# The last layer of a two-layer model: one SiLU and the attention outputs change places with their neighbours in ScalarE's, PE's and VectorE's order

## The chip, the cores and the metric

The kernel runs on one core of a Trainium2 chip. The metric is the time of one execution on the device in microseconds, the median of three runs. The engines that matter here are PE (TensorE, matmuls), ScalarE (ACT), VectorE (DVE) and GpSimd (POOL). Each runs its own list of instructions in order and waits on semaphores for the others.

## The reference, cut to what matters

The model takes 16 x 128 tokens of width 256 through two layers. Layer 0 is a long convolution with gating and a mixture of 16 experts; the change does not touch it. Layer 1, the last, is an attention over features and a feed-forward layer with a low-rank part for each expert:

```python
scaled = einsum('bsd,bse->bde', q, k) / sqrt(256)        # q: the normalized x; k = v: the context
out = einsum('bde,bse->bsd', softmax(scaled, axis=1), v)
x = x + out
# feed-forward, x normalized; the two best of 8 experts (e0, e1), weights rw
for k in range(2):
    x1 = x @ W1.T + B1[e_k] @ (A1[e_k] @ x);  x3 = the same with W3, A3, B3
    x2 = silu(x1) * x3
    out = out + (x2 @ W2.T + B2[e_k] @ (A2[e_k] @ x2)) * rw[k]
x = x + out
```

## The kernel before, in words

`tail_phase` (line 1323) computes the last layer. The 2048 tokens are 8 groups of 256 tokens (two tiles of 128), and the 896 hidden features are 7 chunks of 128, so there are 56 chunk steps. All engines run through one list of steps S, from -7 to 59, with g = S // 7 and n = S % 7, and in each step they work on parts of several chunks. While the chunks of group g are computed, the attention and the routing of group G = g + 1 are spread over the same seven steps (`attention_group`, line 1312 and after). "Group G" below is always the group whose attention is worked on: group 1 in steps 0 to 6, group 2 in steps 7 to 13, up to group 7 in steps 42 to 48. Group 0 is done before the first chunk and the change does not touch it.

What a chunk F needs, with the lines of the profile's rows:

- PE: `base(F)`, 12 matmuls of L1438, products that both picks share; `low_rank(F, kind)`, 12 matmuls of L1453 for each of the two picks, which are added to the base products in the same PSUM bank (kind 0 in step F, kind 1, "the second kind", in step F + 1); `terms` (12 of L1485) and `down` (6 of L1499) in step F + 2.
- ScalarE: `silu(F, k)`, L1624; `hidden_high(F)`, the rounded parts hid_hi, L1630 and L1634.
- VectorE: `product(F, k)`, L1944; `hidden_low(F)`, the rests hid_lo, L1950.
- GpSimd: `weight(F, k)`, L1744; `both(F)`, L1749.

The matrices are split into a high and a low part. For the weights of the chunks of group 0 that happens in the first steps: `high_weights` on ScalarE (L1617) and `low_weights` on VectorE (L1819), two units in each of the steps 1 to 4. base(F) of the first group waits for 2 (F + 2) low units, so base(2) waits for unit 7, the first of step 1, and base(3) for unit 9, the first of step 2.

What group G adds to the steps:

- n = 0: PE `scores(G)` (L1525), n = 1: VectorE `find_top` (L1847), ScalarE `exponentials(G)`, four activations (L1656), VectorE `find_inverse` and `scale_context` (L1852, L1860), PE `attention_out(G)`, 8 matmuls (L1535), which wait for each tile's scaled context.
- n = 2: VectorE `masked_terms` (L1958, for the group whose chunks just ended) and `add_attention(G)` (L1867, then statistics L1872 and L1875); GpSimd `terms_sum` (L1760), `router_rstd(G)` (L1765, L1767), which waits for these statistics, then the step's gathers (`gathers`, L1724), then `weight(S-1, 1)` and `both(S-1)`; ScalarE `terms_high` (L1647), between silu(S-1, 1) and silu(S, 0); VectorE `terms_low` (L1963) and `router_input(G)` (L1884), both behind product(S, 0) and ahead of `hidden_low(S-1)`; PE `low_rank_out` (L1512), which waits for terms_low, and `turn(G)` (L1543), which waits for router_input.
- n = 3 to 6: transposed inputs, the router's logits, its picks and the expert masks.

masked_terms, terms_sum, terms_high, terms_low and low_rank_out exist only from step 9 on, so not in group 1. Exponentials and SiLU are in different activation tables; each change between them is an ACT_TABLE_LOAD, which has the line of the activation behind it.

The order of all of this is written out by hand in the five engines' loops over S. PE's wait for the second kind of chunk F is that product(F, 0) is done; base(F) waits for product(F - 2, 1), because it reuses the bank.

Of the kernel before, what the change touches and what calls it, by code (L numbers as in the profile page):

```python
# [1311 lines left out]
def low_units(S):  # L1312

    return {-6: (4,), -5: (5,), 0: (6,), 1: (7, 8), 2: (9, 10), 3: (11, 12), 4: (13, 14), 5: (15,)}.get(S, ())


def attention_group(S):

    group = S // FB + 1
    return group if 0 <= group < NG else None  # L1320


def tail_phase(nc, memory, a, stage, slots_dram, out_rows, ident, x_sb, comb_idx, norm, w_hi, w_lo, ctx_ring, banks):
# [33 lines left out]
    with ExitStack() as s:  # L1357
# [27 lines left out]
        def is_chunk(F):  # L1385
            return 0 <= F < LAST_CHUNK
# [34 lines left out]
        def _(pe):  # L1421
# [156 lines left out]
            for S in range(FIRST_STEP, END_STEP):  # L1578
                g, n = S // FB, S % FB
                G = attention_group(S)  # L1580
                if is_chunk(S) and S >= EARLY_BASE:
                    base(S)
                if is_chunk(S - 1):
                    low_rank(S - 1, 1)
                if is_chunk(S):
                    low_rank(S, 0)
                if n == 6 and G is not None and G > 0:
                    low_rank_in(G)
                if is_chunk(S - 2):
                    terms(S - 2, SECOND)  # L1590
                    terms(S - 2, BOTH)
                    down(S - 2)
                if n == 2 and 1 <= g <= NG:
                    low_rank_out(g - 1)
                if G is not None:
                    if n == 0:
                        scores(G)
                    if n == 1:
                        attention_out(G)
                    if n == 2:  # L1600
                        turn(G)
                    if n == 3:
                        logits(G)
                    if n == 3 and G == 0:
                        low_rank_in(0)
                        base(0)
                    if n == 5:
                        spread_picks(G)
                    if n == 5 and G == 0:
                        base(1)  # L1610

        @block.scalar
        def _(act):
            def high_weights(k):
                if k >= STAGE_SLOTS:
                    act.wait_ge(staged[k % STAGE_SLOTS], 16 * (k // STAGE_SLOTS))
                nc.scalar.copy(w_hi[:, W_CHUNK[k // 2], (k % 2) * W_COLS:(k % 2 + 1) * W_COLS],  # L1617
                               stage[:, k % STAGE_SLOTS, :]).then_inc(hi_split, 1)

            def silu(F, k):  # L1620
                act.wait_ge(second_done if k else first_done, F + 1)
                if F >= 2:
                    act.wait_ge(lo_done, 2 * (F - 1))
                nc.scalar.activation(f[:, F % 2, k, :], x_banks[F % 2][:, 0:GT], ACT.Silu).then_inc(silu_done, 1)  # L1624

            def hidden_high(F):
                act.wait_ge(weighted, 2 * F + 2)
                if F >= 2:
                    act.wait_ge(terms_done[SECOND], F - 1)
                nc.scalar.copy(hid_hi[:, F % 2, SECOND, :], f[:, F % 2, 1, :]).then_inc(hi_done, 1)  # L1630
                act.wait_ge(both_done, F + 1)
                if F >= 2:
                    act.wait_ge(down_done, F - 1)
                nc.scalar.copy(hid_hi[:, F % 2, BOTH, :], f[:, F % 2, 0, :]).then_inc(hi_done, 1)  # L1634

            def inputs_high(g, u):
                kind, w = u // 2, u % 2
                act.wait_ge(am_mul, 4 * g + u + 1)
                if g >= 1:
                    act.wait_ge(second_done if kind else first_done, FB * g)  # L1640
                nc.scalar.copy(am_hi[:, kind, w, :], mix[:, w, :]).then_inc(am_hi_done, 1)

            def terms_high(g):
                act.wait_ge(t_sum, g + 1)
                if g >= 1:
                    act.wait_ge(out_done, g)
                nc.scalar.copy(t_hi[:, :, :], mix[:, 0, :].rearrange("p (h t) -> p h t", h=HALVES)).then_inc(t_hi_done, 1)  # L1647

            def exponentials(G):
                for k in range(TG):  # L1650
                    b = TG * G + k
                    act.wait_ge(top_done, b + 1)
                    if G >= 1:
                        act.wait_ge(att_done, G)
                    for m in range(HALVES):
                        nc.scalar.activation(weights[:, k, m, :], att_banks[k][:, m * DIM:(m + 1) * DIM], ACT.Exp,  # L1656
                                             bias=minus_top[:, b, m:m + 1],
                                             accum_out=total[:, b, m:m + 1]).then_inc(exp_done, 1)

            def turned_copies(G):  # L1660
                act.wait_ge(turned, G + 1)
                if G >= 1:
                    act.wait_ge(logits_done, G)
                    act.wait_ge(x_low, G)
                nc.scalar.copy(x_t[:, :, :], att_banks[1][:, :].rearrange("p (c t) -> p c t", c=HALVES))\
                  .then_inc(xt_copied, 1)
                act.wait_ge(xt_copied, G + 1)
                if G >= 2:
                    act.wait_ge(second_done, FB * (G - 1))
                nc.scalar.copy(x_hi[:, G % 2, :, :], x_t[:, :, :]).then_inc(x_hi_done, 1)  # L1670

            def picks_copies(G):
                for kind in range(PICKS):
                    act.wait_ge(masks_spread, PICKS * G + kind + 1)
                    if G >= 2:
                        act.wait_ge(t_mul, 2 * (G - 1))
                    nc.scalar.copy(masks_sb[:, G % 2, kind, :], att_banks[kind][:, :]).then_inc(masks_copied, 1)
                act.wait_ge(rw_spread, G + 1)
                if G >= 2:
                    act.wait_ge(weighted, 2 * FB * (G - 1))  # L1680
                nc.scalar.copy(rw_sb[:, G % 2, :, :], out_banks[G % 2][:, :].rearrange("p (k t) -> p k t", k=PICKS))\
                  .then_inc(rw_copied, 1)

            nc.scalar.activation(warm[:, :], minus_half[:, 0:1], ACT.Exp)
            for k in range(STAGE_SLOTS):
                high_weights(k)
            for S in range(FIRST_STEP, END_STEP):
                g, n = S // FB, S % FB
                G = attention_group(S)
                if G is not None:  # L1690
                    if n == 1:
                        exponentials(G)
                    if n == 3:
                        turned_copies(G)
                    if n == 4:
                        act.wait_ge(exp_ready, G + 1)
                        nc.scalar.activation(probs[:, :, :], probs[:, :, :], ACT.Exp).then_inc(probs_exp, 1)
                    if n == 6:
                        picks_copies(G)
                if n == 0 and 0 <= g < NG:  # L1700
                    inputs_high(g, 0)
                    inputs_high(g, 1)
                if is_chunk(S - 1):
                    silu(S - 1, 1)
                if n == 0 and 0 <= g < NG:
                    inputs_high(g, 2)
                if n == 2 and 1 <= g <= NG:
                    terms_high(g - 1)
                if is_chunk(S):
                    silu(S, 0)  # L1710
                if n == 0 and 0 <= g < NG:
                    inputs_high(g, 3)
                if is_chunk(S - 1):
                    hidden_high(S - 1)
                for k in low_units(S):
                    high_weights(k)
# [88 lines left out]
        def _(dve):  # L1805
# [136 lines left out]
            def product(F, k):  # L1942
                dve.wait_ge(silu_done, 2 * F + k + 1)
                nc.vector.tensor_tensor(f[:, F % 2, k, :], f[:, F % 2, k, :], x_banks[F % 2][:, GT:2 * GT], ALU.mult)\  # L1944
                  .then_inc(prod_done, 1)
# [40 lines left out]
            for S in range(FIRST_STEP, END_STEP):  # L1986
                g, n = S // FB, S % FB
                G = attention_group(S)
# [10 lines left out]
                        find_top(b)  # L1999
                if n == 2 and after:  # L2000
                    masked_terms(g - 1)
                if n == 2 and G is not None:
                    add_attention(G)
                if n == 3 and after:
                    add_out(g - 1)
# [5 lines left out]
                    router_picks(G)  # L2011
                if is_chunk(S - 1):
                    product(S - 1, 1)
                if of_group:
                    inputs_product(g, 3)
                if n == 1:
# [95 lines left out]
```

## Time and profile before

| what | value |
|---|---|
| three runs | 795.66, 794.29, 795.27 us |
| median | 795.27 us |
| profiled execution | span 793.3 us from the first to the last instruction; no other time of it is given |
| mean granted TensorE clock | 0.956 of full |
| PE busy | 714.6 us (90%) |
| VectorE, GpSimd, ScalarE busy | 543.9 (69%), 443.1 (56%), 342.5 (43%) us |
| the last layer's chunk steps | from about 335 us to the end |

The span is 1.97 us below the median; what the profile shows is compared with its own span, and the difference is then applied to the median. Starts in the timelines are microseconds from the first instruction. Rows with xN merge N instructions of one form that lie side by side; the bracket at a row's end is the idle time of that engine before it and what ended it.

### The profile page before, as it was taken

Reading aid. Unit: us, or ns where it says so; the run is one execution under the profiler, and the core shown is the slowest. Engines: PE = TensorE matmul, PEld = TensorE weight load, DVE = VectorE, ACT = ScalarE, POOL = GpSimd, SP = SyncE. Lnnn points to the kernel's source line nnn. Section 1 sums busy time; section 2 is a strip of 40 time slices with the busy share of each in tenths; the row PEclk is TensorE's granted clock in tenths of the full one; section 3 lists DMA queues with packets and bytes.
Section 4 is the critical chain, followed back from the end, with each engine's and each line's share of the span. In section 5 each row is a group of like instructions: output and inputs, shape, how many; then the busy total and the mean of one; then the engine's idle time right before and its main releaser. Section 6 shows DMA issues by size and latency. Waiting matters only on the chain.

```text
span 793.3 us, 14732 instructions
## 1 busy us (share of the span) xinstructions
PE 714.6 (90%) x5217; PEld 652.3 (82%) x5217; DVE 543.9 (69%) x1278; ACT 342.5 (43%) x698; POOL 443.1 (56%) x532
## 2 busy tenths in 40 slices
PE   4899988959999981769899999999999999999996
PEld 2444567848999980658899999999999999999996
DVE  4999987975666644676667677677676586755533
ACT  2564533244666652164353344344444534443221
POOL 5877956047766605565276466474664773443532
PEclk9999998988999995689999999999999999999998
DMA  7675615946866864414012021020020110000000
GB/s 248 192 162 137 140 40 120 212 103 186 230 193 196 163 151 123 150 54 146 1 34 62 1 60 36 11 57 28 15 67 14 31 51 1 2 14 2 2 14 14
DMA packets 44599, 68.67 MB, mean 87 GB/s; under 512 B 7376, under 2 KB 32240, under 8 KB 44528
## 3 DMA queue, kind: packets, MB, share of 16 engines
q0 software_dynamic: 10080, 28.72, 17.0%
q1 hardware_dynamic: 34352, 38.97, 15.5%
q8 instruction: 44, 0.72, 0.4%
q14 instruction: 27, 0.22, 0.1%
q10 hardware_dynamic: 96, 0.04, 0.0%
HBM read 50.77 MB, written 14.84 MB: 83 GB/s over the span
## 4 chain that ended last, share of the span: by engine, by line
PE 52%; DVE 4%; POOL 3%; ACT 2%; issue 2%; POOLq 0%; DVEq 0%
PE psum L1453 19%; PE psum L1438 9%; PE psum L1485 9%; PE psum L1499 4%; PE psum L1471 2%; PE psum L1535 2%; PE psum L1525 2%; PE psum L1512 2%; POOL rows_back L1724 1%; PE psum L1553 1%; PE psum L1573 1%; DVE lora_w_lo L1819 1%; PE psum L1543 1%; ACT lora_w_hi L1617 0%; POOL hid L1744 0%
## 5 line engine op out<-in xcount | busy, mean ns | idle before, releaser
L1744 POOL TENSOR_TENSOR hid<-hid,rw_sb 128x256 f32<-128x256 f32 x112 | 93.3, 833 | 153.2 <-DVE hid L1944 152.9
L1453 PE MATMUL psum<-am_hi,lora_w_hi 128*128 128x256 f32 x448 | 127.4, 284 | 2.5 <-DVE am_lo L1939 2.2
L1453 PE MATMUL psum<-am_hi,lora_w_lo 128*128 128x256 f32 x448 | 127.2, 284 | 0.0
L1453 PE MATMUL psum<-am_lo,lora_w_hi 128*128 128x256 f32 x448 | 127.1, 284 | 0.0
L1944 DVE TENSOR_TENSOR hid<-hid,psum 128x256 f32<-128x256 f32 x112 | 46.8, 418 | 116.4 <-ACT hid L1624 115.2
L1624 ACT ACTIVATE hid<-psum 128x256 f32<-128x256 f32 x112 | 42.4, 385 | 177.2 <-PE psum L1453 177.0
L1043 POOL DMA_INDIRECT rows_in<-y_scratch,slot_token x80 | 76.2, 952 | 31.8 <-issue 27.1
L1724 POOL DMA_INDIRECT rows_back<-slots_scratch,comb_idx x64 | 66.6, 1040 | 39.8 <-POOLq L707 24.2
L1453 PEld LDWEIGHTS psum<-am_hi,lora_w_hi 128*128 128x128 f32 x448 | 85.9, 192 | 3.1 <-POOL am_lo L1755 3.1
L1950 DVE TENSOR_TENSOR hid_lo<-hid,hid_hi 128x256 fp32r<-128x256 f32 x112 | 74.1, 682 | 19.4 <-ACT hid_hi L1630 14.4
L1453 PEld LDWEIGHTS psum<-am_lo,lora_w_hi 128*128 128x128 f32 x448 | 86.0, 192 | 0.0
L1453 PEld LDWEIGHTS psum<-am_hi,lora_w_lo 128*128 128x128 f32 x448 | 85.9, 192 | 0.0
L1438 PE MATMUL psum<-lora_x_hi,lora_w_hi 128*128 128x256 f32 x224 | 67.7, 302 | 4.0 <-DVE lora_w_lo L1819 4.0
L327 POOL TENSOR_TENSOR kv<-ctx_t 128x1024 f32<-128x1024 f32 (+2 forms) x48 | 57.5, 1290 | 11.3 <-PE psum L448 11.3
L1485 PE MATMUL psum<-hid_hi,lora_w_hi 128*128 128x256 f32 x224 | 62.9, 281 | 0.7 <-DVE hid_lo L1950 0.7
L1438 PE MATMUL psum<-lora_x_lo,lora_w_hi 128*128 128x256 f32 x224 | 62.9, 281 | 0.0
L1438 PE MATMUL psum<-lora_x_hi,lora_w_lo 128*128 128x256 f32 x224 | 62.8, 280 | 0.0
L1485 PE MATMUL psum<-hid_lo,lora_w_hi 128*128 128x256 f32 x224 | 62.6, 279 | 0.0
L1485 PE MATMUL psum<-hid_hi,lora_w_lo 128*128 128x256 f32 x224 | 62.5, 279 | 0.0
L883 PE MATMUL psum<-moe_w_hi,moe_xt_hi 128*128 x160 | 49.5, 310 | 0.0
L1438 PEld LDWEIGHTS psum<-lora_x_hi,lora_w_hi 128*128 128x128 f32 x224 | 42.7, 191 | 5.2 <-DVE lora_w_lo L1819 4.8
L591 DVE TENSOR_TENSOR prod<-psum,q_t 128x1024 f32<-128x1024 f32 (+1 forms) x64 | 41.2, 685 | 8.2 <-PE psum L448 5.9
(255 smaller groups left out, 2147.7 us busy)
## 6 DMA issues: line engine op xcount, KB each, us to landing
slots_scratch<-y_out SPq DMA_DIRECT2D x40, 256.0 KB, 3.4
stage<-in_moe_weights SPq DMA_DIRECT2D x18, 384.0 KB, 3.7
moe_w_lo<-in_moe_weights POOLq DMA_DIRECT2D x18, 384.0 KB, 7.0
lora_stage_early<-in_lora_weights SPq DMA_DIRECT2D x16, 384.0 KB, 3.8
x_sb<-in_x SPq DMA_DIRECT2D x4, 512.0 KB, 6.1
ctx_t<-in_ctx_t SPq DMA_DIRECT2D x4, 512.0 KB, 7.4
y_scratch<-y SPq DMA_DIRECT2D x8, 256.0 KB, 2.6
x_sb<-shared_out POOLq DMA_DIRECT2D x4, 512.0 KB, 5.1
```

The source lines that it names most:

```text
L327: last = nc.gpsimd.tensor_tensor(kv[:, n % KV_SLOTS, :, first:first + shape[2] * shape[3]].rearrange("p n (i j) -> p n i j", j=shape[3]), ...
L591: last = nc.vector.tensor_tensor(prod[:, :, j, i], y_ji, query[:, :, i].unsqueeze(2).broadcast_to(shape), ALU.mult)
L883: last = nc.tensor.matmul(gu_banks[q % 2][:, k * DIM:(k + 1) * DIM], xp, wp, start=(c == 0 and j == 0), stop=(c == HALVES - 1 and j == 2))
L1043: nc.gpsimd.indirect_dma_start(out=rows_in[:, i % ROW_SLOTS, :], out_offset=None, in_=y_dram[:, :], in_offset=bass.IndirectOffsetOnAxis(ap ...
L1438: nc.tensor.matmul(x_banks[F % 2][:, w * GT:(w + 1) * GT], wp, xp, start=(w == 0 and c == 0 and k == 0), stop=False, skip_group_check=True)
L1453: last = nc.tensor.matmul(x_banks[F % 2][:, w * GT:(w + 1) * GT], wp, ap, start=False, stop=(half == 1 and k == 2), skip_group_check=True)
L1485: last = nc.tensor.matmul(term_banks[which][:, half * GT:(half + 1) * GT], wp, hp, start=(n == 0 and half == 0 and j == 0), stop=(n == FB ...
L1624: nc.scalar.activation(f[:, F % 2, k, :], x_banks[F % 2][:, 0:GT], ACT.Silu).then_inc(silu_done, 1)
L1724: nc.gpsimd.indirect_dma_start(out=rows_back[:, t % ROW_TILES, k * DIM:(k + 1) * DIM], out_offset=None, in_=slots_dram[:, :], in_offset=ba ...
L1744: nc.gpsimd.tensor_tensor(f[:, F % 2, k, :], f[:, F % 2, k, :], rw_sb[:, F // FB % 2, k, :], ALU.mult)\
L1944: nc.vector.tensor_tensor(f[:, F % 2, k, :], f[:, F % 2, k, :], x_banks[F % 2][:, GT:2 * GT], ALU.mult)\
L1950: nc.vector.tensor_tensor(hid_lo[:, F % 2, which, :], f[:, F % 2, 1 - which, :], hid_hi[:, F % 2, which, :].bitcast(FP32), ALU.subtract).t ...
```

## The change

On PE, `attention_out(G)` of groups 1 to 7 moves from the end of step n = 1 to step n = 2, behind base(S) and ahead of the second kind of the chunk before. On ScalarE, `exponentials(G)` of these groups move behind silu(S - 1, 1) in step n = 1. On VectorE, `add_attention(G)` moves behind product(S - 1, 1) in step n = 2. Group 0 keeps the old order. No instruction's size changes.

```diff
@@ PE
                 if is_chunk(S) and S >= EARLY_BASE:
                     base(S)
+                if n == 2 and G is not None and G > 0:
+                    attention_out(G)
                 if is_chunk(S - 1):
                     low_rank(S - 1, 1)
...
                     if n == 0:
                         scores(G)
-                    if n == 1:
+                    if n == 1 and G == 0:
                         attention_out(G)
@@ ScalarE
                 if G is not None:
-                    if n == 1:
+                    if n == 1 and G == 0:
                         exponentials(G)
...
                 if is_chunk(S - 1):
                     silu(S - 1, 1)
+                if n == 1 and G is not None and G > 0:
+                    exponentials(G)
@@ VectorE
                 if n == 2 and after:
                     masked_terms(g - 1)
-                if n == 2 and G is not None:
+                if n == 2 and G == 0:
                     add_attention(G)
...
                 if is_chunk(S - 1):
                     product(S - 1, 1)
+                if n == 2 and G is not None and G > 0:
+                    add_attention(G)
```

## Rows read from the trace of the kernel before

**Rows 1.** busy time in the stretch of steps 14 to 20 (columns: stretch, length, PE, PEld, DVE, ACT, POOL, PEclk, DMA share, GB/s)

```profile
455.00:510.00 55.00, 55.00 (x460) 54.36 (x459) 38.54 (x88) 23.43 (x51) 32.94 (x39) 1.00 0.12 35
```

**Rows 2.** timeline of PE, steps 1 to 5 (columns: start, us, engine, line, operation)

```profile
347.45 0.28 PE L1453 MATMUL psum<-am_lo,lora_w_hi 128*128 128x256 f32 x1
...
353.44 3.75 PE L1535 MATMUL psum<-att_weights,att_scaled 128*128 128x256 f32 x8 [4.15 <-DVE att_scaled L1860]
...
365.76 0.38 PE L1438 MATMUL psum<-lora_x_hi,lora_w_hi 128*128 128x256 f32 x1 [0.88 <-DVE lora_w_lo L1819]
...
374.23 0.38 PE L1438 MATMUL psum<-lora_x_hi,lora_w_hi 128*128 128x256 f32 x1 [1.07 <-DVE lora_w_lo L1819]
...
383.36 0.39 PE L1438 MATMUL psum<-lora_x_hi,lora_w_hi 128*128 128x256 f32 x1 [0.98 <-DVE lora_w_lo L1819]
```

**Rows 3.** timeline of ScalarE, steps 1 and 2

```profile
348.13 0.48 ACT L1656 ACTIVATE att_weights<-psum,att_minus_top 128x256 f32<-128x256 f32 x1 [0.73 <-DVE att_minus_top L1847]
...
350.08 1.28 ACT L1624 ACT_TABLE_LOAD   x1
351.37 0.66 ACT L1624 ACTIVATE hid<-psum 128x256 f32<-128x256 f32 x2
...
360.79 0.39 ACT L1624 ACTIVATE hid<-psum 128x256 f32<-128x256 f32 x1 [5.00 <-PE psum L1453]
```

**Rows 4.** timeline of VectorE, steps 1 and 2

```profile
352.32 1.84 DVE L1860 TENSOR_SCALAR att_scaled<-ctx_ring,att_inverse 128x128 f32<-128x128 f32 x4
...
355.62 1.82 DVE L1819 TENSOR_TENSOR lora_w_lo<-lora_stage_early,lora_w_hi 128x768 fp32r<-128x768 f32 x2
357.35 0.67 DVE L1867 TENSOR_TENSOR x_sb<-x_sb,psum 128x512 f32<-128x512 f32 x1
...
361.21 0.42 DVE L1944 TENSOR_TENSOR hid<-hid,psum 128x256 f32<-128x256 f32 x1 [2.18 <-ACT hid L1624]
...
362.98 1.19 DVE L1884 TENSOR_SCALAR lora_y<-x_sb,meanvar,rstd 128x256 f32<-128x256 f32 x2
```

**Rows 5.** timeline of GpSimd, step 2

```profile
359.12 0.23 POOL L1765 TENSOR_SCALAR rstd<-meanvar 128x2 f32<-128x2 f32 x1 [3.71 <-DVE meanvar L1875]
359.43 0.72 POOL L1767 TENSOR_TENSOR rstd<-rstd,minus_half 128x2 f32<-128x2 f32 x1
360.34 1.05 POOL L1724 DMA_INDIRECT rows_back<-slots_scratch,comb_idx  x1 [0.18 <-issue]
361.72 0.73 POOL L1744 TENSOR_TENSOR hid<-hid,rw_sb 128x256 f32<-128x256 f32 x1 [0.33 <-DVE hid L1944]
```

**Rows 6.** busy time and granted clock in three short stretches (columns as Rows 1)

```profile
351.75:352.00 0.25, 0.00 (x0) 0.00 (x0) 0.21 (x1) 0.25 (x2) 0.00 (x0) 0.61 0.84 328
...
358.50:359.00 0.50, 0.50 (x5) 0.50 (x5) 0.50 (x3) 0.00 (x0) 0.00 (x0) 0.87 1.05 381
...
375.50:376.00 0.50, 0.50 (x6) 0.50 (x5) 0.00 (x0) 0.48 (x2) 0.00 (x0) 0.70 0.76 190
```

**Rows 7.** timeline of PE, steps 15 and 16

```profile
471.22 1.89 PE L1535 MATMUL psum<-att_weights,att_scaled 128*128 128x256 f32 x8
...
474.32 0.28 PE L1453 MATMUL psum<-am_hi,lora_w_hi 128*128 128x256 f32 x1
...
479.29 0.28 PE L1512 MATMUL psum<-lora_w_hi,t_hi 128*128 128x256 f32 x1
```

**Rows 8.** timeline of ScalarE, step 16

```profile
475.94 0.39 ACT L1624 ACTIVATE hid<-psum 128x256 f32<-128x256 f32 x1 [3.94 <-PE psum L1453]
476.22 0.61 ACT L1647 CAST t_hi<-mix 128x512 fp32r<-128x512 f32 x1
```

**Rows 9.** timeline of VectorE, step 16

```profile
473.30 1.27 DVE L1958 TENSOR_TENSOR mix<-psum,masks_sb 128x512 f32<-128x512 f32 x2
...
478.13 0.99 DVE L1963 TENSOR_TENSOR t_lo<-mix,t_hi 128x512 fp32r<-128x512 f32 x1
```

**Rows 10.** timeline of GpSimd, step 16

```profile
474.65 1.29 POOL L1760 TENSOR_TENSOR mix<-mix 128x512 f32<-128x512 f32 x1 [1.56 <-DVE mix L1958]
```

## Prediction

> **What bounds the kernel now.** I read the page first: PE is busy for 714.6 of 793.3 us, and the chain that ended last is mostly PE's matmuls of the last layer. That says where the time is, not where the change can act, so I cut the last layer in two with the view of busy time by stretch and the timelines. From about 402 us PE never pauses: in the stretch of steps 14 to 20 it is busy for 55.00 of 55.00 us at the full clock [rows 1]. This holds for groups 2 to 7, six groups of seven steps. Taking a wait out there can bring nothing; putting one in costs its full length. Before 402 us, in group 1, PE does pause: 4.15 us ahead of the attention outputs, and ahead of each base(3), base(4), base(5) for VectorE's low weight parts (L1819) [rows 2]. Steps 1 to 6 are a ring: base(S) and low_rank on PE, SiLU, product, GpSimd's weight and both, the hid_hi and hid_lo parts, high_weights, low_weights, base(S + 1). Whatever is added to the ring in group 1 moves everything behind it.
>
> **Step 1, ScalarE and VectorE.** No operation is added or removed, and there are two table loads as before: exponentials, then SiLU, 1.28 us each. What moves: silu(0,1) may start when low_rank(0,1) ends, 347.45 + 0.28, so at 347.8 instead of 351.37 [rows 2, 3]. Behind it: 0.39 us, exp load 1.28, four exponentials with their accumulators 1.95 (348.13 to 350.08), SiLU load 1.28, silu(1,0). The exponentials end at 351.4, 1.35 us later than now; silu(1,0) ends at 353.1. VectorE's four scalings (1.84 us [rows 4]) wait for the exponentials and two reciprocals of some 0.1 us, and end at 353.5 instead of 354.16. What follows them, product(1,0) and the two hid_lo parts, takes 1.5 us (354.16 to 355.62), then the first low weight unit half of 1.82. So unit 7, the last that base(2) needs, is ready at 355.9 instead of 356.5.
>
> **Step 2, PE.** Now the attention outputs fill 353.44 to 357.2 while base(2) would be held for its weights until 356.5 anyway [rows 2, 4]. They are nearly hidden there. After the change PE is idle from 349.3 to 355.9, then base(2), then the outputs, then low_rank(1,1). The clock fell to the 1.2 GHz level at 351.85 after 2.5 us of idle PE and came back at about 358.6, 5.2 us after PE had resumed [rows 6]. At the full clock 42 matmuls take 4.97 us [rows 7], so the twelve of base(2) take 1.4, and the outputs 1.6 of their 1.89 until the next matmul starts; at the low one they take about 2.7 and 3.75. I take the clock back at the same moment, 358.6 (lower bound of the cold work: 2.7 us; upper: the 5.2 us seen). Then base(2) ends at 358.6, the outputs at 360.2, and silu(1,1) comes 1.62 us after low_rank starts (474.32 to 475.94 in step 16 [rows 7, 8]), at 361.8 instead of 360.79: 1.0 late, with bounds 0.5 and 2.3.
>
> **Step 2, VectorE and GpSimd: the largest term.** add_attention now stands behind product(1,1), but GpSimd's order is unchanged: router_rstd(1), one gather, and only then weight(1,1). From the addition to the first reciprocal-root instruction are 1.77 us (357.35 to 359.12), from there to the gather's end 2.27 (360.34 + 1.05 less 359.12) [rows 4, 5]. Today all that is over when product(1,1) ends at 361.63, and weight(1,1) follows at 361.72, 0.09 later. After: 1.77 + 2.27 and some gaps, 4.1 us later. Downstream 0.3 us is forgiven, because today the hid_lo parts of this step wait behind router_input (1.19 us from 362.98), which then fits under GpSimd's work. So base(3), now 4.13 us behind product(1,1), comes 7.8 behind it: +3.7. With the 1.0 above, base(3) moves from 365.76 to 370.5.
>
> **Steps 3 to 6.** PE now has two pauses before base(3), the longer some 3 us, so it will probably run at the low clock: silu(2,1) then comes up to 2.4 us later relative to base(3), of which about 0.8 was waiting on VectorE and GpSimd anyway: +1.5. Against that, the clock today falls at 375.65, just after base(4), and slows that step [rows 6]; base(4) to base(5) took 9.13 us against 8.47 for the step before [rows 2]. With PE fed almost without pause ahead of base(4), that is not repeated: -1.2. Step 5 is held by VectorE's router picks and moves along. Group 1: 1.0 + 3.7 + 1.5 - 1.2 = **+5.0 us**. Bounds: 3.0 (no cold stretch at base(3), the one at base(4) gone), 7.5 (the late clock in step 2 and at base(3), with nothing given back).
>
> **Groups 2 to 7.** Take group 3, steps 14 to 20; the others repeat it. In step 15 low_rank(14,1) starts at 466.25: the 42 matmuls from low_rank(15,1) at 474.32 to 479.29 take 4.97 us, and the same 42 lie before 471.22 [rows 7]. So silu(14,1) is ready at 467.87; with 0.39, 1.28, 1.95 the exponentials end at 471.5, the scalings at 472.6 for the first tile and 473.5 for the second. PE, having done base(16), asks for them at 472.6 and 473.5: at most 0.1 us lost. But VectorE is now late: product(15,0) and hid_lo until 475.05, so masked_terms starts there instead of at 473.30 [rows 9]. It takes 1.27, GpSimd's sum 0.08 later 1.29 [rows 10], the t_hi part 0.61 [rows 8], and silu(16,0) stands behind that on ScalarE, product(16,0) behind silu(16,0), t_lo (0.99) behind the product: 476.3, 477.7, 478.35, 478.65, 479.1, 480.0. PE wants it at 479.29 + 0.1; today it is ready at 479.12, so only 0.17 us of slack is there. A wait of 0.6. The router's z arrives at 481.1 to 481.6, when PE asks at 481.4: 0 to 0.2. I take 0.65 us for a group, bounds 0.3 and 0.9; six groups make **+3.9 us** (1.8 to 5.4). GpSimd's weight(15,1) also comes 2.4 us later, but terms(15) is due only after base(17) and two low_ranks, 5.6 us further on; that stays hidden.
>
> In this sum each switch of table costs one load, since SiLU starts 0.01 us after the load ends (350.08 + 1.28, then 351.37 [rows 3]). The Trainium skill, ScalarE: Activation LUTs, section What ACT_TABLE_LOAD costs, gives about 1.28 us for the load, with which the row agrees, and a drain of about 1.38 us behind it, which the rows don't show. By that rule a switch would cost 2.66 us and the sum would be some 15 us larger; the trace speaks against it.
>
> **Sum.** 5.0 + 3.9 = 8.9 us: the span goes from 793.3 to 802.2. The median of the runs, 795.27, is 1.97 above the span of the profiled execution, so I predict 804.2 us. A measurement of this kernel can tell about 0.2%, 1.6 us, from no change.
>
> **The rivals.**
> - *Group 1 alone loses.* If terms_low comes half a us sooner than I have it (its duration 0.7 instead of 0.99, masked_terms moved up), the slack of 0.17 suffices: 795.3 + 5.0 = 800.3 us. For it: I count every link at today's value under contention. Against: three links are fixed waits.
> - *The groups alone lose.* If GpSimd's late weight(1,1) falls into a wait that is there anyway, the time is 795.3 + 3.9 = 799.2. Against: base(3) waits for VectorE's weights today, so there is no such cover.
> - *The clock makes it dearer.* Every step of group 1 runs partly at 1.2 GHz: another 2.4 us in step 3 and 1.2 in step 4, together with the upper bound of the groups: 807 to 810 us. For it: a 4.15 us wait grows to 6.6.
> - *Dear switches.* Each of the two switches stops ScalarE for twice the length of a load, 2.56 instead of 1.28 us. Then in six groups the exponentials end 1.3 and silu(15,0) 2.6 us later than in my walk, t_lo follows, and PE waits about 2.4 us more in each: 804.2 + 14 = 818 us. Against it stand the 0.01 us between load and SiLU [rows 3]. The rule of the Trainium skill named above is what speaks for it.
> - *It does not matter.* Attention is off the chain and the new waits overlap with PE's pauses: 795.3. For it: in groups 2 to 7 the slacks are within half a us of enough. Against: group 1.
> - *Faster.* SiLU no longer stands behind exponentials, base(2) starts at 355.9 instead of 357.2, the outputs run at the full clock in 1.6 us instead of 3.75, and the cold stretch after base(4) vanishes: 0.3 us from the first two and 1.2 from the last, 793.8 us. It decides only if weight(1,1) is not held, that is if less than 1.5 of the 3.7 us reaches base(3), and if t_lo's slack suffices. The order in GpSimd's program speaks against it.
>
> **How the numbers follow.** Forecast as summed 0.62; group 1 alone 0.11; the groups alone 0.05; dearer clock 0.10; dear switches 0.01; no matter 0.07; faster 0.04. The likeliest case with its bounds goes from 800.0 to 808.2 (4.8 to 12.9 us added); to reach the groups-alone case I go down to 799.0, and take half of the dearer one with 809.0. Slower by over 0.2%: 0.62 + 0.11 + 0.05 + 0.10 + 0.01 = 0.89; same 0.07; faster 0.04.
>
> **What would show it.** In the profile after: a pause of PE ahead of base(2) of about 6.6 us, in place of 4.15 ahead of L1535; weight(1,1) (L1744) about 4.1 us behind product(1,1); base(3) near 370.5, base(5) near 388.5, and the first chunk of group 1 about 5 us late; the stretch of 55 us no longer full, with PE waiting about 0.6 us for t_lo (L1963) ahead of L1512 once in each of six groups; the chain passing through GpSimd and VectorE there. The forecast is wrong if weight(1,1) follows product(1,1) at once, if t_lo is ready before PE asks, or if PE's waits in group 1 shrink.

## The result, and the profile after

The changed kernel takes 804.03 us (median of 4 runs, 802.42 to 806.16) against 794.78 us for the kernel before on the same chip; the ratio is 1.0122, 95% interval 1.01 to 1.0145. The forecast was 804.2 us. By the medians the kernel grew by 9.25 us, where 8.9 were forecast on a median of 795.27. The profiled execution has a span of 802.5 us, 9.2 more than before. PE is busy for 715.8 us, 1.2 more than before, so nearly all of it is waiting.

Who PE waited for between 340 and 403 us, in the profile after:

```profile
PE psum L1438 <- DVE lora_w_lo L1823: 12.1, 5, 6.5
...
PE psum L1543 <- DVE lora_y L1888: 1.5, 1, 1.5
```

Before, PE's pause of step 1 ended with the scaled context [rows 2]; now there is none ahead of L1535, and the base matmuls wait 12.1 us in all for the low weight parts, 6.5 of them in one piece. The timeline of PE, steps 2 to 5:

```profile
356.10 0.58 PE L1438 MATMUL psum<-lora_x_hi,lora_w_hi 128*128 128x256 f32 x1 [6.50 <-DVE lora_w_lo L1823]
...
370.92 0.58 PE L1438 MATMUL psum<-lora_x_hi,lora_w_hi 128*128 128x256 f32 x1 [2.90 <-DVE lora_w_lo L1823]
...
381.11 0.38 PE L1438 MATMUL psum<-lora_x_hi,lora_w_hi 128*128 128x256 f32 x1 [0.41 <-DVE lora_w_lo L1823]
...
388.92 0.38 PE L1438 MATMUL psum<-lora_x_hi,lora_w_hi 128*128 128x256 f32 x1 [1.20 <-DVE lora_w_lo L1823]
```

base(3) is at 370.92, forecast 370.5; base(5) at 388.92, forecast near 388.5. The timeline of VectorE in step 2, which answers to [rows 4]:

```profile
362.75 0.42 DVE L1948 TENSOR_TENSOR hid<-hid,psum 128x256 f32<-128x256 f32 x1 [5.84 <-ACT hid L1626]
363.09 0.68 DVE L1871 TENSOR_TENSOR x_sb<-x_sb,psum 128x512 f32<-128x512 f32 x1
...
365.93 1.38 DVE L1888 TENSOR_SCALAR lora_y<-x_sb,meanvar,rstd 128x256 f32<-128x256 f32 x2 [0.85 <-POOL rstd L1771]
```

And of GpSimd, which answers to [rows 5]:

```profile
364.87 0.23 POOL L1769 TENSOR_SCALAR rstd<-meanvar 128x2 f32<-128x2 f32 x1 [9.97 <-DVE meanvar L1879]
...
366.08 1.05 POOL L1728 DMA_INDIRECT rows_back<-slots_scratch,comb_idx  x1 [0.18 <-issue]
367.17 0.73 POOL L1748 TENSOR_TENSOR hid<-hid,rw_sb 128x256 f32<-128x256 f32 x1
```

product(1,1) ends at 363.17. GpSimd has stood still for 9.97 us in front of router_rstd, then does that and the gather, and starts weight(1,1) at 367.17: 4.00 us behind the product, where it was 0.09.

To set the runs beside each other I use starts in the timelines of PE: of the first base matmul (base(0)), of base(2), of low_rank(1,1), of base(3), (5), (7), (49), and the end of the last matmul. What lies ahead of base(0) differs between two executions by a few us, whatever the kernel (base(0) at 333.0 to 339.0), so this length compares the edits better than the spans do. Each row of the table is one execution, the profiled one.

| us | base(0)-(2) | (2)-low_rank(1,1) | low_rank(1,1)-(3) | (3)-(5) | (5)-(7) | (7)-(49) | (49)-end | whole |
|---|---|---|---|---|---|---|---|---|
| before | 21.12 | 2.52 | 6.61 | 17.60 | 18.33 | 330.41 | 57.94 | 454.53 |
| after | 20.19 | 4.42 | 10.40 | 18.00 | 18.33 | 333.38 | 58.65 | 463.37 |
| only_group1 | 20.65 | 5.64 | 10.40 | 17.08 | 18.33 | 330.38 | 57.45 | 459.93 |
| only_groups | 21.52 | 2.05 | 6.81 | 17.82 | 18.32 | 332.20 | 57.36 | 456.08 |
| scalar_only | 20.89 | 2.50 | 6.60 | 16.24 | 18.32 | 337.89 | 57.36 | 459.80 |
| no_scalar | 20.73 | 4.45 | 10.40 | 18.00 | 18.31 | 334.05 | 57.35 | 463.29 |
| add_first | 20.26 | 4.35 | 8.24 | 17.18 | 18.32 | 332.16 | 58.34 | 458.85 |
| rstd_behind | 20.82 | 5.78 | 8.14 | 18.24 | 18.31 | 333.50 | 58.64 | 463.43 |
| gather_first | 20.96 | 5.63 | 9.15 | 17.17 | 18.37 | 336.27 | 58.60 | 466.15 |
| kept_busy | 20.32 | 3.03 | 10.43 | 18.15 | 18.36 | 333.31 | 58.10 | 461.70 |
| weights_first | 20.71 | 1.56 | 6.50 | 14.54 | 17.42 | 330.44 | 58.35 | 449.52 |
| weights_first_after | 20.32 | 4.52 | 8.26 | 15.98 | 17.36 | 335.01 | 58.66 | 460.11 |
| filled | 14.78 | 4.22 | 6.62 | 15.81 | 17.36 | 330.57 | 57.66 | 447.02 |

The whole grew by 8.8 us: 5.2 ahead of base(7), 3.0 from there to base(49), 0.7 behind it. The last column but one varies from 57.4 to 58.7 with no relation to the edits, so its 0.7 is not put down to the change.

What one execution can tell has limits. only_groups and add_first were profiled in the fastest of their six executions (794.62 and 797.79 us, medians 798.70 and 801.31), kept_busy, no_scalar and gather_first in their slowest. The kernel before has in its profile a low clock in step 4 (a mean of 0.50 from 376 to 378 us) which scalar_only and weights_first, with the same matmuls there, do not have (1.00 from 374 to 380 us); this is worth about 1.3 us (base(4) to base(5) 7.79 us in scalar_only, 9.13 before). So a stretch of the table shows a mechanism where the rows beside it do, and a difference of a microsecond or two of the whole needs the ratio of all executions.

### The profile page after: what moved, and what is told of

It reads as the page before. It is cut to its first block, busy times and chain, and to the rows that moved or that the text cites. A ratio compares the mean times of both kernels' runs of the same rounds, so it can differ in the third digit from the quotient of the medians.

```text
span 802.5 us, 14732 instructions
## 1 busy us (share of the span) xinstructions
PE 715.8 (89%) x5217; PEld 653.9 (81%) x5217; DVE 536.6 (67%) x1278; ACT 340.9 (42%) x698; POOL 445.3 (55%) x532
## 4 chain that ended last, share of the span: by engine, by line
PE 51%; DVE 5%; POOL 3%; ACT 2%; issue 1%; POOLq 0%; DVEq 0%
PE psum L1453 19%; PE psum L1438 10%; PE psum L1485 8%; PE psum L1499 4%; PE psum L1471 3%; PE psum L1525 2%; PE psum L1535 2%; PE psum L1512 1%; POOL rows_back L1728 1%; PE psum L1573 1%; DVE lora_w_lo L1823 1%; DVE lora_y L1888 1%; POOL rstd L1771 1%; PE psum L1553 1%; PE psum L1543 1%
## 5 line engine op out<-in xcount | busy, mean ns | idle before, releaser
L1748 POOL TENSOR_TENSOR hid<-hid,rw_sb 128x256 f32<-128x256 f32 x112 | 91.6, 818 | 154.3 <-DVE hid L1948 154.0
L1954 DVE TENSOR_TENSOR hid_lo<-hid,hid_hi 128x256 fp32r<-128x256 f32 x112 | 76.0, 695 | 28.5 <-ACT hid_hi L1632 22.2
L1438 PE MATMUL psum<-lora_x_hi,lora_w_hi 128*128 128x256 f32 x224 | 67.2, 300 | 12.1 <-DVE lora_w_lo L1823 12.1
L327 POOL TENSOR_TENSOR kv<-ctx_t 128x1024 f32<-128x1024 f32 (+2 forms) x48 | 57.4, 1289 | 11.4 <-PE psum L448 11.4
L1632 ACT CAST hid_hi<-hid 128x256 fp32r<-128x256 f32 x56 | 22.6, 403 | 58.6 <-POOL hid L1748 58.6
```

What stands on the lines that cost most here:

```text
L327: last = nc.gpsimd.tensor_tensor(kv[:, n % KV_SLOTS, :, first:first + shape[2] * shape[3]].rearrange("p n (i j) -> p n i j", j=shape[3]), ...
L1438: nc.tensor.matmul(x_banks[F % 2][:, w * GT:(w + 1) * GT], wp, xp, start=(w == 0 and c == 0 and k == 0), stop=False, skip_group_check=True)
L1748: nc.gpsimd.tensor_tensor(f[:, F % 2, k, :], f[:, F % 2, k, :], rw_sb[:, F // FB % 2, k, :], ALU.mult)\
L1954: nc.vector.tensor_tensor(hid_lo[:, F % 2, which, :], f[:, F % 2, 1 - which, :], hid_hi[:, F % 2, which, :].bitcast(FP32), ALU.subtract).t ...
```

## The experiments

The theory under test: group 1 loses because GpSimd's weight(1,1), part of the ring, waits behind router_rstd for statistics that now come late; the later groups lose a little because the router's z and t_lo come just too late. The main rival: the attention outputs on PE's path, and the low clock behind the longer pause, are the loss, and GpSimd's hold is hidden.

**only_group1 and only_groups: where it is lost.** In both, the conditions `G == 0` and `G > 0` of the changed kernel are altered on all three engines:

```diff
-                if n == 2 and G is not None and G > 0:
+                if n == 2 and G == 1:            # only_groups: G > 1
                     attention_out(G)
```

> The change for group 1 alone, groups 2 to 7 in the old order. Two terms theory: group 1 loses in its ring (base(3) near 370.9, scores(2) about 5.5 us later than before), PE waits for nothing in groups 2 to 7; about 5.5 us over the kernel before. If instead the loss were spread evenly over the seven groups: about 1.3 us.

> The change for groups 2 to 7 alone. Two terms theory: steps 0 to 6 as before (base(3) at 365.8), then 0.2 to 0.8 us in each of six groups ahead of low_rank_out and turn, 3.0 us in all, 798 us. If the six groups only passed on what group 1 did to the phase of the work: 795 us.

Measured: ratios 1.0083 (1.0054 to 1.0112) and 1.0071 (1.0048 to 1.0095). By the table only_group1 is 5.4 us longer than before, with (7) to (49) unchanged; only_groups leaves everything ahead of base(7) within a us and takes 1.8 us more in the six groups. The loss has two places. How it divides is less sure: by the medians only_groups costs 5.0 us (798.70 for 793.66; 3.8 to 7.5 by the interval), more than the 1.6 of its profiled execution, and only_group1 7.1, which together are more than the 9.25 of the whole change. In the profiles the six groups lose 1.8 us here and 3.0 with the whole change; a later section shows what these 1.2 us are.

**scalar_only and no_scalar: whose move it is.** scalar_only has the kernel before with ScalarE's part of the change, no_scalar the change without it:

```diff
+                if n == 1 and G is not None and G > 0:   # scalar_only; left out in no_scalar
+                    exponentials(G)
```

> Only ScalarE's part: exponentials(G) behind silu(S-1,1), PE and VectorE in the old order. The length from the first base matmul to the last matmul is 454.5 us before and 463.4 with the whole change. My theory: group 1 is as before or 0.4 us shorter (its ring is untouched), and in groups 2 to 7 PE, which asks for the scaled context 5.0 us after low_rank starts, gets it 5.9 after: 0.9 us a group; 459.8 us. If the later exponentials cost nothing without the other moves: 454.5.

> PE's and VectorE's part, exponentials where they were. My theory: GpSimd's hold in step 2 stays, so group 1 loses all of its 5 us (base(2) to base(3) 14 to 15 us instead of 9.1), and masked_terms is early again, so groups 2 to 7 lose at most 0.1 us each; 460 us by the same measure. If ScalarE's order were the cause in group 1: 455 to 457.

scalar_only: ratio 1.0094 (1.0073 to 1.0115), whole 459.80, the forecast figure. Its group 1 is even 1.6 us shorter than before, most of it between base(3) and base(5) (16.24 for 17.60), where the clock does not fall in this execution. PE's waits in its steps 8 to 48:

```profile
PE psum L1535 <- DVE att_scaled L1862: 5.2, 6, 0.9
```

The shape is as expected, though the six groups lose 7.5 us, not 5.4. The waits are 0.86 us in each group; t_lo took 1.31 or 1.32 us in groups 3, 4 and 6, which are 56.5 us long, and 0.68 to 0.73 in the others, which are 56.1. no_scalar: ratio 1.014 (1.0116 to 1.0163); group 1 has exactly the stretches of the whole change (4.45, 10.40, 18.00), so ScalarE's order has no part in that loss. But the six groups lose 3.6 us where I expected nearly nothing. Its waits there:

```profile
PE psum L1543 <- DVE lora_y L1886: 2.0, 5, 0.6
```

That is `turn`, which waits for router_input in five of the six groups: my expectation looked at t_lo and forgot that the later addition makes z late too.

**add_first, rstd_behind and gather_first: GpSimd's hold.** In add_first VectorE adds the attention in front of product(S-1,1), as before the change. rstd_behind does router_rstd(1) behind weight(1,1) and both(1). gather_first does the step's gather while GpSimd waits anyway:

```diff
 # add_first, VectorE
-                if n == 2 and G == 0:
+                if n == 2 and G is not None:
                     add_attention(G)
...
                     product(S - 1, 1)
-                if n == 2 and G is not None and G > 0:
-                    add_attention(G)
...
 # rstd_behind, GpSimd
                     both(S - 1)
+                if n == 2 and G == 1:
+                    router_rstd(G)
...
 # gather_first, GpSimd
+                if n == 2 and S >= 0:
+                    gathers(S)
                 if n == 2 and G is not None:
                     router_rstd(G)
...
-                gathers(S)
+                if n != 2 or S < 0:
+                    gathers(S)
```

> The change, but VectorE's add_attention stays ahead of product(S-1,1). My theory (GpSimd's weight(1,1) is held by router_rstd, which waits for the addition's statistics): add_attention now runs while PE does low_rank(1,1), weight(1,1) comes 1.3 us behind product(1,1) instead of 4.1, base(3) is 2.8 us earlier, and the router's z is in time in groups 2 to 7; 799.5 us, 4.5 less than the change. Rival (the attention outputs on PE's path and the low clock are the loss, GpSimd's hold is hidden): within 1 us of the change, 803 to 805.

> The change, but in group 1 GpSimd does router_rstd behind weight(1,1) and both(1). My theory: weight(1,1) follows product(1,1) at once (now 4 us later), the hid parts of this step are then held by VectorE's router_input instead, base(3) is 1.8 us earlier than with the change (33.2 instead of 35.0 us behind the first base matmul), and the whole 461.6 us. If GpSimd's order did nothing: 35.0 and 463.4.

> The change, with GpSimd's gather of step n = 2 ahead of router_rstd. It is then issued while GpSimd waits for the statistics. Group 1, my theory: weight(1,1) is held 1.25 us less, so from the first matmul of low_rank(1,1) to base(3) 9.2 us instead of 10.4. Groups 2 to 7: PE's wait for the router's z comes from VectorE's router_input, 0.73 us where GpSimd leaves it alone and 1.4 to 1.6 where they run side by side; with weight(S-1,1) now right beside it, it should be long in all six groups: steps 7 to 48 take 334.5 to 335.5 us instead of 333.4 (330.4 before the change). If the two engines don't slow each other, 333.4 or less, as GpSimd has less ahead of it.

The stretch from low_rank(1,1) to base(3) is the one in question. It is 10.40 us with the change, 8.24 in add_first, 8.14 in rstd_behind, 9.15 in gather_first (9.2 expected), 6.61 before. Three different edits of the hold each shorten it, and the rival, which needed it unchanged, falls as the explanation of this stretch. In rstd_behind weight(1,1) follows its product at once, 0.08 us behind it:

```profile
362.28 0.74 POOL L1748 TENSOR_TENSOR hid<-hid,rw_sb 128x256 f32<-128x256 f32 x1 [8.59 <-DVE hid L1950]
```

The 1.5 us that are left there above the 6.61 are VectorE's: router_input, which waits for router_rstd, ends at 366.10 us, and hidden_low(1) and the low weights stand behind it. The ratios: add_first 1.0095 (1.0072 to 1.0119), rstd_behind 1.0105 (1.008 to 1.013), gather_first 1.0138 (1.011 to 1.0166). Their intervals overlap with that of the whole change (1.01 to 1.0145), so it is the traces that show the effect of the hold, not the times of the kernel. The gain does not reach the whole in full. In rstd_behind it is lost again: base(2) to low_rank(1,1) is 5.78 instead of 4.42, because the attention outputs there ran at the low clock for 3.40 us instead of 2.04, and base(2) came 0.6 late:

```profile
356.49 3.40 PE L1535 MATMUL psum<-att_weights,att_scaled 128*128 128x256 f32 x8
```

only_group1 and gather_first show the same 1.2 us, with no edit there that could cause it (gather_first's is behind it). In the profile after, the granted clock is back at 359.1 us, 3.0 behind the start of base(2); in only_group1 it is back at 361.1, 5.5 behind. So when the clock comes back, relative to the work, is different from one profiled execution to the next, and is worth over 1 us in this stretch. rstd_behind as a whole (463.43) therefore missed its 461.6.

**The router's z, and VectorE beside GpSimd.** gather_first lost 5.9 us in the six groups, which I had expected to be 4.1 to 5.1; I had counted 1.4 to 1.6 us for router_input. Its router_input and GpSimd's work beside it, in the timelines of group 3:

```profile
486.20 1.63 DVE L1891 TENSOR_SCALAR lora_y<-x_sb,meanvar,rstd 128x256 f32<-128x256 f32 x2 [0.62 <-POOL rstd L1771]
```

```profile
486.14 0.73 POOL L1748 TENSOR_TENSOR hid<-hid,rw_sb 128x256 f32<-128x256 f32 x1
486.95 0.73 POOL L1753 TENSOR_TENSOR hid<-hid 128x256 f32<-128x256 f32 x1
```

It took 1.62 or 1.63 us in all six groups. In the changed kernel the same two instructions, with a gather beside them, take 0.73 us in groups 2, 3 and 5 and 1.39, 1.39 and 1.63 in groups 4, 6 and 7; the timelines of VectorE, groups 3 and 4:

```profile
485.83 0.73 DVE L1888 TENSOR_SCALAR lora_y<-x_sb,meanvar,rstd 128x256 f32<-128x256 f32 x2 [0.62 <-POOL rstd L1771]
...
541.10 1.39 DVE L1888 TENSOR_SCALAR lora_y<-x_sb,meanvar,rstd 128x256 f32<-128x256 f32 x2 [0.62 <-POOL rstd L1771]
```

And what PE waits for `turn` in group 4:

```profile
542.54 0.65 PE L1543 MATMUL psum<-ident,lora_y 128*128 128x128 f32 x4 [0.33 <-DVE lora_y L1888]
```

From base to base, groups 2 to 7 of the changed kernel take 55.28, 55.27, 55.78, 55.24, 55.79 and 56.02 us, against 55.05 (55.19 in the last) before: 0.2 us where router_input is short, 0.7 to 0.8 where it is long. In only_groups five of six are short, which are the 1.2 us between 1.8 and 3.0. It is not group 1 that decides: with group 1 changed too, rstd_behind has three long ones and weights_first_after six. What decides between short and long with a gather beside it was not found out.

**kept_busy: the clock.** 52 matmuls without use ahead of base(2) and 22 ahead of base(3), written to banks that are free at that time:

```diff
+                if S == 2:
+                    pe.wait_ge(am_mul, 4)
+                    keep_busy(term_banks[0], 52)
                 if is_chunk(S) and S >= EARLY_BASE:
                     base(S)
...
                         turn(G)
+                        if G == 1:
+                            pe.wait_ge(x_added, 2)
+                            keep_busy(att_banks[0], 22)
```

> The change, with 52 matmuls without use in PE's pause ahead of base(2) and 22 in the one ahead of base(3), so that the clock stays up. My theory: base(2) and base(3) still start when VectorE's weights are there (356.1 and about 369.6), but run at the full clock; low_rank(1,1) ends 1.3 us sooner, low_rank(2,1) another 1 to 1.5; 801.5 us, 2.5 less than the change. Rival (the clock is most of group 1's loss): 5 us less, 799. If the clock is nothing: 804.

The ratio is 1.0128 (1.0107 to 1.0149), no gain that can be seen in the times. In the profile base(2) to low_rank(1,1) is 3.03 instead of 4.42, the 1.4 us expected. The second part came to nothing: the clock stayed up at base(3) and fell a step later instead, in the stretch 381 to 387 us:

```profile
381.00:387.00 6.00, 5.43 (x33) 5.43 (x34) 2.00 (x6) 3.42 (x5) 0.00 (x0) 0.72 0.23 68
```

so (3) to (5) is 18.15 instead of 18.00. In this execution the clock was 1.4 us of group 1's length; it is not the loss, since the stretch from low_rank(1,1) to base(3) stayed at 10.43.

**weights_first, weights_first_after, filled: the ring, and a faster kernel.** If group 1 is a ring through the weight parts, these should be moved out from behind the hid parts:

```diff
+                for k in low_units(S):
+                    low_weights(k)          # and high_weights likewise on ScalarE
                 if is_chunk(S - 1):
                     hidden_low(S - 1)
-                for k in low_units(S):
-                    low_weights(k)
```

> The kernel before the change, with high_weights ahead of hidden_high on ScalarE and low_weights ahead of hidden_low on VectorE. My theory: group 1 is a ring through the weights, so taking them out from behind the hid parts shortens each of steps 2 to 6 by 0.5 to 1.2 us; 3 us less in all, 451.5 us by the same measure, about 791.5 for the kernel. If PE's pauses in group 1 have another cause: no gain.

> The whole change, and the weight parts ahead of the hid parts as in weights_first. From the first matmul of low_rank(1,1) to base(3) are 6.6 us before the change, 10.4 with it, 8.1 to 8.2 with GpSimd's hold shortened in either way. My theory (the hold costs because the ring through the weights passes behind the hid parts): with the weights out of it only router_input stands before them, 7.8 us; from the first base matmul to the last matmul 457.5 us instead of 463.4. If the hold reached base(3) by another way: 10 us again.

weights_first, made of the kernel before, has a ratio of 0.9969 (0.995 to 0.9988) and is 5.0 us shorter by the table, 3.1 of them between base(3) and base(5). About 1.3 of these, as much as in scalar_only, are the low clock of step 4 that this profile does not have, and by the medians the gain is 2.1 us. In weights_first_after, made of the changed kernel (ratio 1.0061, 1.0039 to 1.0083), the stretch from low_rank(1,1) to base(3) falls from 10.40 to 8.26, expected 7.8. The whole is 460.1 and not 457.5; 1.6 of the difference is router_input, which was long in all six groups (335.01 for 333.38). filled adds, for group 1 alone, the order of the change where it fits: units 7 and 8 are split ahead of everything in step 1, silu(0,1) comes before the exponentials, base(2) before the attention outputs, and add_attention stays in its old place.

```diff
 # ScalarE; VectorE has low_weights behind product(0, 1)
+                if S == 1:
+                    for k in low_units(S):
+                        high_weights(k)
...
                     silu(S - 1, 1)
+                if S == 1:
+                    exponentials(1)
 # PE
                     base(S)
+                if S == 2:
+                    attention_out(1)
```

> weights_first, and in group 1 alone what was sound in the change: silu(0,1) ahead of the exponentials and the attention outputs behind base(2), but with units 7 and 8 split before both, so that base(2) fills PE's pause, and with VectorE's add_attention in its old place. Groups 2 to 7 as before. My theory: base(2) starts some 6 us earlier than before, low_rank(1,1) 4 us earlier, 445.5 us by the same measure, about 787 for the kernel (ratio 0.991). If the pause of step 1 only moves elsewhere (VectorE is then the bound of group 1): 449.5, as weights_first.

The timeline of PE in filled:

```profile
351.09 0.39 PE L1438 MATMUL psum<-lora_x_hi,lora_w_hi 128*128 128x256 f32 x1 [0.36 <-DVE lora_w_lo L1826]
...
353.70 1.97 PE L1535 MATMUL psum<-att_weights,att_scaled 128*128 128x256 f32 x8 [0.96 <-DVE att_scaled L1867]
```

The pauses ahead of base(2) and of the outputs are 0.36 and 0.96 us, together 1.3 instead of 4.15 before and 6.50 with the change. The ratio is 0.9917 (0.99 to 0.9934), 788.34 us against 794.45: faster than both kernels. By the table it is 447.0 us, between the 445.5 and the 449.5 of the expectation. base(3) comes 25.6 us behind base(0), where it was 28.8 in weights_first and 30.3 before; 1.3 of these 3.2 us are given back between base(3) and base(5), 15.81 against 14.54, so the theory held for the pause and was too hopeful for what follows it. That VectorE is the bound there was not tested.

## Why the prediction was right

Point by point, with the starts shifted by the 0.4 us by which base(0) is later in the profile after.

- *Step 1, ScalarE and VectorE.* silu(0,1) started at 348.20 (347.8 + 0.4 forecast), the four exponentials took 1.95 us with their accumulators, base(2) started at 356.10 (355.9 + 0.4). Right. The four scalings took 1.34 us for the 1.84 assumed, but product(1,0) then waited for its SiLU, so that only 0.2 us of it arrived.
- *The switch of tables.* Before the exponentials the load began at 348.60 and the first of them at 349.89, 0.01 us behind its end, after a SiLU that it follows:

```profile
348.20 0.39 ACT L1626 ACTIVATE hid<-psum 128x256 f32<-128x256 f32 x1 [1.79 <-PE psum L1453]
348.60 1.28 ACT L1658 ACT_TABLE_LOAD   x1
349.89 0.47 ACT L1658 ACTIVATE att_weights<-psum,att_minus_top 128x256 f32<-128x256 f32 x1
```

  The rival of dear switches is out.
- *Step 2, PE and the clock.* silu(1,1) at 362.34 for a forecast of 361.8 + 0.4. The moment of the clock's return that I chose, 358.6 + 0.4, was right for this execution (359.1), and that is in part luck: only_group1 and gather_first show a later one, 1.2 us dearer; it was inside the bounds.
- *GpSimd's hold, the largest term.* 4.00 us measured for 4.1, base(3) 7.75 us behind product(1,1) for 7.8: 3.8 us of growth from low_rank(1,1) to base(3) for 3.7. The experiments show that the hold is the larger part of this growth (2.2 to 2.3 of 3.8 us go with it in add_first and rstd_behind), that in rstd_behind the rest is router_input on VectorE, and that ScalarE's move has no part in it.
- *Steps 3 to 6.* Forecast +0.3 in sum, +0.4 measured (18.00 for 17.60). The parts hold too: base(3) to base(4) 10.19 us for 8.47 (+1.5 forecast), base(4) to base(5) 7.81 for 9.13 (-1.2 forecast). It is a cold stretch that changes its place: the clock was low until about 376 us, and full from then on, where before it fell at 375.65. That PE, fed without pause, is what kept it up in step 4 is not shown: in scalar_only, with PE's order of before, that step took 7.79 us as well.
- *Groups 2 to 7.* Forecast 3.9 us, measured 3.0, and the inside of this term was off. I had t_lo 0.6 us late and z nearly in time. In fact t_lo is about 0.2 us late (in group 3 it ends at 485.21 and L1512 starts at 485.26), and z is late by another half us in three of six groups. The wait of 0.6 us for t_lo that I named as a sign is not in the profile: the view of PE's waits from 400 to 745 us has only L1543, 1.2 us in three waits. The step that was mis-sized is "I count every link at today's value": the four scalings took 0.88 us, not 1.87, since GpSimd stood still beside them in the new order (from 476.1 to 479.5 us in group 3); t_lo took 0.68, not 0.99, and it was GpSimd's power of router_rstd beside it that became longer, 1.18 for 0.72; router_input took 0.73 or 1.39 to 1.63. My sign of a stretch of 55 us that is no longer full shows only in the groups with a long router_input: the stretch 518 to 573 us has PE busy for 54.67 us, group 3 still for 55.00.
- *The end.* 0.7 us behind base(49) were not forecast; the other runs show that this stretch varies so by itself.

The sum was 8.9 us, the table gives 8.8. Of that, 0.7 is the end's, and 0.9 less came from the groups, so the agreement of the totals is closer than that of the terms. It is the mechanism and the order of the terms that the runs bear out; that the total agrees to a fifth of a microsecond is luck, as two profiled executions can differ by more than a microsecond in the clock alone.

## What to carry to other kernels

Before an operation is moved back on one engine, look in the program of every engine that waits for it at what stands behind that wait: here the one multiplication on which the ring of all engines turned had followed its product by 0.09 us and then followed it by 4.00, because an operation that waits for the moved statistics stood in front of it. Where PE is full, such a move can only cost; where it pauses, fill the pause with work whose inputs can be made early (here base(2), with its weights split earlier: -0.8% in filled), rather than moving the waiting work behind it. And when durations of VectorE and GpSimd are carried over into a new order, ask whether the two still run side by side.

## What the runs showed of the hardware

VectorE's fp32 operations with one factor per row (L1860 and router_input) take about twice as long while GpSimd does elementwise work beside them: 1.87 for 0.88 us, and 1.63 (gather_first) for 0.73. The four scalings in the kernel before and in scalar_only, which differ in nothing that they compute:

```profile
414.93 1.87 DVE L1860 TENSOR_SCALAR att_scaled<-ctx_ring,att_inverse 128x128 f32<-128x128 f32 x4
```

```profile
471.29 0.88 DVE L1862 TENSOR_SCALAR att_scaled<-ctx_ring,att_inverse 128x128 f32<-128x128 f32 x4
```

1.87 us when GpSimd's weight and both run beside them, 0.88 when it idles (all six groups of scalar_only). GpSimd's power in router_rstd took 0.72 us in the kernel before [rows 5] and 1.18 beside VectorE's t_lo in the changed one. The Trainium skill says in SBUF — State Buffer, section SBUF: two separate sides, that GpSimd and certain VectorE operations share one pair of ports, and that whichever starts first keeps the other out for the whole instruction. These durations agree with it; the ports themselves are in no trace. In gather_first it costs up to 0.8 us a group; whether it is also the cause of the three long groups of the changed kernel, where only a gather runs beside router_input, is not shown.

The other surprise is how little the clock could be bought back: 74 extra matmuls kept it up through two pauses, and it fell in the next step instead (a mean of 0.72 from 381 to 387 us in kept_busy).
